# First layer's routing, row turning and scatter moved inside the recurrence, one block of 128 tokens per turn, with the turns of all engines written out

## Chip, core and metric

The kernel runs on one core of one Trainium2 chip. The metric is the device time of one execution in microseconds (us). TensorE is PE (its weight loads PEld), VectorE is DVE, ScalarE is ACT, GpSimd is POOL, SyncE is SP.

## What is computed

Four layers on x (8 batches, 512 tokens, 256 features). Only the first layer matters here: a recurrence (GRU) over 512 time steps, whose hidden states are the input of a mixture of 8 experts, two of which work on each token. The rest is cut.

```python
def step(h, inp):                       # _L0_cond_ref, scanned over t = 0..511, h is 8 x 256
    x_t, prop = inp
    comb = jnp.concatenate([x_t, h], axis=-1)
    z = jax.nn.sigmoid(comb @ Wz + bz)
    r = jax.nn.sigmoid(comb @ Wr + br)
    comb2 = jnp.concatenate([x_t, r * h], axis=-1)
    h_cand = jnp.tanh(comb2 @ Wh + bh)
    h_new = (1.0 - z) * h + z * h_cand
    h_next = jnp.where(prop, jnp.tanh(h_new @ Wp + bp), h_new)   # prop: every 4th step
    return (h_next, h_new)
# _L0_ffn_ref: logits = y @ gate_w + gate_b, the two largest of 8 per token, softmax of the two,
# out = sum of gate * (gelu(y @ w1[e] + b1[e]) @ w2[e] + b2[e]) over the token's two experts
x = x + _L0_ffn_ref(_L0_cond_ref(x, cond_1024, ...), ...)
x = x + _L1_ffn_ref(_L1_cond_ref(x, ...), ...)   # and two more layers
```

## The kernel before, in words

Everything lies in one program with a block per engine; the order on each engine is the order in the code, and semaphores join the engines.

**Recurrence.** 512 steps, in 32 turns (TURNS) of 16 (STEPS). Hidden states are kept with the features on the partitions, so a step's moving operand is 8 columns wide (the batches). Each value is held as two f16 parts. In one step PE multiplies h by the weights of gates r and z (`recur`, 24 matmuls, line 1546), ACT takes the tanh of r and of z (L669, L671), DVE makes r times h in parts (L996, L997, L999) and the mixing factors (L1002, L1003, L1005), PE does the candidate (12 matmuls), ACT its tanh (L673), and DVE's scan L1012 makes the new h, L1013 the same in f32 into `hist`, L1015 the low part. Each fourth step (CHUNK) adds a fourth product, an ACT tanh (L678) and `split_entry` (L983, L984, L986). While PE waits for c, it does one piece of the next turn's input projections (`projections`: a bias matmul, L1526 or L1534, or an f32 product with x, L1530). PE's turns are written out in the program; those of DVE, ACT (two at a time) and POOL are hardware loops (Fori). POOL copies `hist`, half a turn at a time, to HT, features by token (L588).

**After the recurrence.** PE makes the gate logits of all 4096 tokens from HT (`logits0`, L1590) and turns them (L1600). DVE picks the two experts for all 32 blocks of 128 tokens at once (`top2`, L1026 to L1032); two matmuls with a strict triangle and with ones count the ranks (`prefixes`); DVE makes `slots`, each token's two rows in the DRAM array tile_rows (L1070 to L1080), and `tile_table` makes `etab`, which tells SP what expert and rows each of the 39 tiles of 256 rows has (L1037 to L1051). Per block, PE turns 128 tokens of HT to rows (L1619), ACT copies them twice into `row_out0` (L719, L720, a ring of GRING = 4 blocks), and POOL scatters them by `slots` with two indirect DMAs (L611). SP waits for all 64 scatters and for `etab`, and loads the first tile's rows (L430) and weights (L389 to L392); then the expert tiles begin (L1654, L1666, with L731 on ACT). In the order of DVE, the router preparation for the second layer (L1084 to L1101) stands between `tile_table` and the expert tiles.

tile_rows is filled with zeros first, by 34 large DMAs of SP (L423, L424), 17 for each of two layers, which count to one semaphore, `xg_zeroed`.

## Time and profile before

| | us |
|---|---|
| median of 3 runs | 3123.79 (3120.74 to 3123.80) |
| profiled execution, its own time | 3125.09 |
| span of its trace | 3123.3 |
| recurrence, step 0 to the last | about 37 to 1293 |
| from there to the first expert matmul | 1293 to 1429 |
| PE busy / DVE busy / ACT busy / POOL busy | 2734.3 / 1386.6 / 863.7 / 406.7 |

The profiled execution is 1.3 us above the median. Its times are from the start of the span. A busy PE in the recurrence is a chain of dependent small matmuls, so the shares of busy time don't say what bounds; the waits do.

### The profile page before, as it was taken

The page shows a single profiled execution, that of the slowest core. Times are in us where ns is not written, and L with a number is a line of the kernel's source. Part 1 is how long each engine was busy: PE and PEld are TensorE (multiplying, and loading weights), DVE is VectorE, ACT ScalarE, POOL GpSimd, SP SyncE. Part 2 cuts the span into 40 slices and gives each one's busy share as a digit, 9 for nine tenths or more (in the row PEclk, how much of TensorE's full clock was granted, in tenths as well). Part 3 has the DMA queues.
Part 4 walks back from the last instruction along what each step waited for, and adds up shares of the span by engine and source line. Part 5 has one row for each costly group of instructions (what it writes and reads, how often), then busy time and mean ns, then how long its engine had stood idle before and what let it go on. Part 6 is the DMA issues. An engine that isn't in the chain of part 4 may idle for free.

```text
span 3123.3 us, 72740 instructions
## 1 busy us (share of the span) xinstructions
PE 2734.3 (88%) x27762; PEld 2069.9 (66%) x27762; DVE 1386.6 (44%) x6799; ACT 863.7 (28%) x2717; POOL 406.7 (13%) x478
## 2 busy tenths in 40 slices
PE   7888888888888888727999999899997999998788
PEld 5777777777777777516888888655784334386477
DVE  5555555555555555400111111366443556743532
ACT  1222222222222222222222222111353332433332
POOL 1000000000000000061111111122341000002233
PEclk6555555555555555658999999899998999999889
DMA  9990000000000000025666666521345321000123
GB/s 314 385 359 23 2 2 2 2 2 2 2 2 2 2 2 2 1 99 182 186 202 189 198 193 196 178 84 57 108 139 182 114 101 56 1 0 0 36 81 101
DMA packets 218189, 295.93 MB, mean 95 GB/s; under 512 B 57673, under 2 KB 160689, under 8 KB 216689
## 3 DMA queue, kind: packets, MB, share of 16 engines
q1 hardware_dynamic: 200624, 243.80, 23.9%
q0 software_dynamic: 17344, 48.78, 4.3%
q8 instruction: 188, 3.08, 0.4%
q14 instruction: 33, 0.26, 0.0%
HBM read 167.59 MB, written 124.94 MB: 94 GB/s over the span
## 4 chain that ended last, share of the span: by engine, by line
PE 76%; DVE 8%; ACT 6%; issue 5%; POOL 3%; DMA 2%; SPq 1%; DVEq 0%; POOLq 0%; ACTq 0%
PE bank L1546 20%; PE bank L1654 9%; PE bank L1666 9%; PE bank L1530 8%; PE bank L1738 4%; ACT gate_r L669 3%; DVE rhpart L996 3%; PE bank L1836 3%; PE bank L1880 3%; PE bank L1938 3%; PE bank L1789 2%; PE bank L1800 2%; POOL tile_rows L611 2%; PE bank L2036 2%; PE bank L2048 2%
## 5 line engine op out<-in xcount | busy, mean ns | idle before, releaser
L1546 PE MATMUL bank<-h_high,WB 128*128 128x8 f16 x9216 | 422.2, 169 | 87.2 <-DVE h_high L1012 67.4
L1546 PEld LDWEIGHTS bank<-h_high,WB 128*128 128x128 f16 x9216 | 335.5, 105 | 204.4 <-DVE h_high L1012 165.9
L1546 PE MATMUL bank<-rhpart,WB 128*128 128x8 f16 x6144 | 288.8, 171 | 84.8 <-DVE rhpart L996 84.8
L1546 PEld LDWEIGHTS bank<-rhpart,WB 128*128 128x128 f16 x6144 | 242.9, 106 | 130.7 <-DVE rhpart L996 128.1
L1654 PE MATMUL bank<-WA,WB 128*128 128x256 f32 x1248 | 310.1, 381 | 7.3 <-DMA WA<-in_L_ffn_b 7.3
L1666 PE MATMUL bank<-WB,hid 128*128 128x256 f32 x1248 | 313.8, 379 | 0.0
L1530 PE MATMUL bank<-XT,WB 128*128 128x128 f32 x792 | 304.6, 481 | 0.0
L1546 PE MATMUL bank<-h_low,WB 128*128 128x8 f16 x4608 | 299.7, 171 | 0.0
L1654 PEld LDWEIGHTS bank<-WA,WB 128*128 128x128 f32 x1248 | 238.7, 191 | 40.6 <-issue 7.7
L731 ACT ACTIVATE hid<-bank,b_up 128x256 f32<-128x256 f32 x312 | 148.0, 474 | 395.6 <-PE bank L1654 395.6
L1666 PEld LDWEIGHTS bank<-WB,hid 128*128 128x128 f32 x1248 | 234.3, 190 | 30.3
L1109 DVE TENSOR_TENSOR y_dest<-WA,pad_row 128x2 uint32<-128x2 f32 x78 | 12.5, 161 | 509.1 <-PE bank L1641 509.1
L669 ACT ACTIVATE gate_r<-bank 128x16 f32<-128x16 f32 x512 | 94.2, 184 | 495.8 <-PE bank L1546 495.8
L598 POOL DMA_INDIRECT expert_rows<-WA,y_dest x156 | 149.6, 959 | 592.1 <-DVE WA L1133 489.3
L1546 PEld LDWEIGHTS bank<-h_low,WB 128*128 128x128 f16 x4608 | 212.9, 106 | 17.3
L1530 PEld LDWEIGHTS bank<-XT,WB 128*128 128x128 f32 x792 | 198.7, 312 | 0.7
L588 POOL TENSOR_TENSOR HT<-GB,unscale 128x128 f32 x64 | 29.8, 466 | 1254.5 <-DVE GB L1013 1254.5
L1012 DVE TENSOR_TENSOR_SCAN h_high<-mix_times,mix_plus 128x32 f16<-128x32 f32 x512 | 115.2, 225 | 152.0 <-ACT mix_plus L673 152.0
L673 ACT ACTIVATE mix_plus<-bank 128x16 f32<-128x16 f32 x512 | 95.4, 186 | 279.4 <-PE bank L1546 279.4
L996 DVE SCALAR_TENSOR_TENSOR rhpart<-gate_r,GB 128x16 f16<-128x16 f32 x384 | 67.3, 175 | 223.0 <-ACT gate_r L669 223.0
L1880 PE MATMUL bank<-hid,WA 128*128 128x512 f32 x256 | 121.2, 607 | 0.0
L1836 PE MATMUL bank<-HT,WA 128*128 128x512 f32 x256 | 119.7, 593 | 0.0
(357 smaller groups left out, 3953.2 us busy)
## 6 DMA issues: line engine op xcount, KB each, us to landing
WB<-in_L_ffn_w SPq DMA_DIRECT2D x78, 1024.0 KB, 7.7
tile_rows<-WA SPq DMA_DIRECT2D x32, 2176.0 KB, 19.4
WA<-tile_rows SPq DMA_DIRECT2D x78, 272.0 KB
GB<-gates SPq DMA_DIRECT2D x8, 2048.0 KB
WA<-expert_rows SPq DMA_DIRECT2D x16, 512.0 KB, 5.4
WB<-expert_rows SPq DMA_DIRECT2D x16, 512.0 KB, 8.3
WA<-in_L_ffn_b SPq DMA_DIRECT2D x40, 128.0 KB, 8.2
GB<-in_x SPq DMA_DIRECT2D x8, 512.0 KB, 7.5
```

Of the source, the lines that this page charges most:

```text
L598: nc.gpsimd.indirect_dma_start(yg, bass.IndirectOffsetOnAxis(ap=y_dest[:, x, s:s + 1], axis=0), yrow[:, x % 2, s], None).then_inc(yrow_sto ...
L669: nc.scalar.activation(flat(gate_r), gate_in(r_bank, s), ACT.Tanh, scale=0.5 / GSCALE).then_inc(r_ready, 1)
L731: nc.scalar.activation(hid0[:, f], banks[f % RING][:, 0:ET], ACT.Gelu, bias=b0_up[:, i, f:f + 1]).then_inc(S["hid_ready"], 1)
L996: nc.vector.scalar_tensor_tensor(rhpart[:, 0], gate_r[:], 1.0, h, ALU.add, ALU.mult).then_inc(rh_part, 1)
L1012: nc.vector.tensor_tensor_scan(h_high[:], mix_times[:], mix_plus[:], 0.0, ALU.mult, ALU.add).then_inc(h_part, 1)
L1530: nc.tensor.matmul(o, wx[:, g, k, m * P:(m + 1) * P], xview[:, k, bass.ds(it * STEPS, STEPS)], start=False, stop=False, skip_group_check=True)
L1546: last = nc.tensor.matmul(bank[:, m * width + s * B:m * width + (s + 1) * B], wpart[:, g, w, k, m * P:(m + 1) * P], part[a][:, k * B:(k + ...
L1654: last = nc.tensor.matmul(banks[f % RING][:, 0:ET], w0_up[i][:, k, f * P:(f + 1) * P], xgT[:, i, k], start=k == 0, stop=k == KD - 1)
L1666: last = nc.tensor.matmul(banks[4 + m][:, 0:D], hid0[:, h, half_of(m)], w0_down[i][:, h], start=h == 0, stop=h == F0 - 1)
L1738: last = nc.tensor.matmul(banks[u % RING][:], (wsh1, wsh3)[u % 2][:, k, u // 2 * P:(u // 2 + 1) * P], XT[:, k, cols(j)], start=k == 0, sto ...
L1836: last = nc.tensor.matmul(banks[f % RING][:], v1[:, f, k], HT[:, k, cols(j)], start=k == 0, stop=k == KD - 1)
L1880: last = nc.tensor.matmul(banks[4 + m][:], v2[:, h, half_of(m)], hid[:, h % RING], start=False, stop=h == E - 1)
```

## The change

The work that followed the recurrence is done block by block inside it. A block is now one turn: 16 steps times 8 batches are 128 tokens, so their order in the blocks is another one (`dest_turn` holds the place of each in the result). In turn `it` the engines work on block `it - 1`:

- POOL makes two copies of each half turn, to HT as before and to `hturn` (in `hid`, a ring of two blocks), and scatters block `it - 2` at the turn's start. The first four scatters are held until turn 5.
- PE does the block's logits in steps 2 and 3 with `hturn` as weights, turns its rows in steps 6 and 7, and the two rank products in steps 12 and 13, all in spare columns of the bank that holds the fourth product. The projection pieces are dealt out anew, so that these steps have a bias piece and not an f32 one.
- DVE does the choice and the placing in pieces of one to three instructions behind steps 4 to 8, 12, 14, 15 and the next turn's step 0, on operands of 8 elements or fewer. `r_base` carries the counts from block to block.
- ACT copies the rows in step 8 and does one tanh in step 11 (the two gates are now a sigmoid of the difference of the two logits, where they were made with an exponential).
- The loops of DVE, ACT and POOL are written out, so their semaphore values are constants. DVE waits for the small loads (`rw_loaded`) and for POOL's constants ahead of the recurrence. POOL makes two more iotas at the start.
- Each layer's zero fill has a semaphore of its own. Behind the recurrence only block 31, the rest of block 30, `tile_table` and the second layer's preparation are left.

The diff, cut to its core (names of semaphores that only count on from another number are left out):

```diff
@@ POOL
-            with pool.Fori(0, TURNS) as it:
+            def scatter_block(b):
+                q = b % GRING
+                pool.wait_ge(slots_ready, b + 1)
+                pool.wait_ge(row_ready, b + 1)
+                for c in range(2):
+                    nc.gpsimd.indirect_dma_start(xg[0], bass.IndirectOffsetOnAxis(ap=slots[:, c, b:b + 1], axis=0),
+                                                 row_out0[:, q, c], None).then_inc(moved[q], 16)
+            def history(it, half):
...
+                if it >= 2:
+                    pool.wait_ge(row_psum, it - 1)
+                pool.wait_ge(h_full, it * STEPS + (half + 1) * n)
+                nc.gpsimd.tensor_tensor(hturn[:, it % 2].rearrange("p k (s b) -> p s k b", b=B)[:, half * n:(half + 1) * n], made, unscale[:],
+                                        ALU.mult).then_inc(hist_copied, 1)
+                nc.gpsimd.tensor_tensor(hview[:, it * STEPS + half * n:it * STEPS + (half + 1) * n], made, unscale[:],
+                                        ALU.mult).then_inc(hist_copied, 1)
+            for it in range(TURNS):
+                if it == GRING + 1:
+                    pool.wait_ge(xg_zeroed[0], ZEROED[0])
+                    for b in range(GRING - 1):
+                        scatter_block(b)
+                if it > GRING:
+                    scatter_block(it - 2)
                 for half in range(2):
+                    history(it, half)
+            for b in range(TURNS - 2, NBLK):
+                scatter_block(b)
@@ ACT, in gru_turn
+                    if it and s == 8:
+                        block_rows(it - 1, p_bank[:, 128:128 + D])
+                    if it and s == 11:
+                        block_gate(it - 1)
@@ DVE
+            def route_block(b, logit_bank, rank_bank, total_bank):
+                q = b % GRING
+                dve.wait_ge(logit_psum, b + 1)
+                V.tensor_tensor(r_log, logit_bank, rbias0[:], ALU.add).then_inc(logits_taken, 1)
+                yield
+                x = r_log
+                for m, mask in ((r_m1, r_mask1), (r_m2, r_mask2)):
...
+                    routed(V.tensor_reduce(m, x, AX_X, ALU.max))
+                    yield
+                    last_routed()
+                    routed(V.scalar_tensor_tensor(r_tmp, x, m, prefer[:], ALU.is_equal, ALU.mult))
+                    yield
+                    last_routed()
+                    routed(V.tensor_reduce(r_p, r_tmp, AX_X, ALU.max))
+                    yield
+                    last_routed()
+                    routed(V.tensor_scalar(mask, r_tmp, r_p, None, ALU.is_equal))
+                    yield
...
+                V.tensor_tensor(r_w, r_mask1, r_mask2, ALU.add).then_inc(masks_ready, 1)
...
+                dve.wait_ge(prefix_psum, b + 1)
+                routed(V.tensor_tensor(r_pos, rank_bank, r_base[:], ALU.add))
...
+            ROUTE_AT = {4: 3, 5: 3, 6: 3, 7: 3, 8: 1, 12: 1, 14: 3, 15: 3}
...
-            with dve.Fori(0, TURNS) as it:
+            dve.wait_ge(rw_loaded, 9 * 16)
+            dve.wait_ge(prefer_ready, 2 * E + 7)
+            dve.wait_ge(const_ready, 11)
...
+            for it in range(TURNS):
+                if it:
+                    routes.append(route_turn(it))
                 for s in range(STEPS):
...
+                    if s == 0 and len(routes) > 1:
+                        for _ in routes[-2]:
+                            pass
+                    if it:
+                        for _ in range(ROUTE_AT.get(s, 0)):
+                            next(routes[-1], None)
@@ PE
+            def beside_step(it, s, bias, inputs, p_bank):
+                if it + 1 < TURNS:
+                    for g, m in {0: ((0, 0), (0, 1)), 2: ((1, 0),), 3: ((1, 1),), 6: ((2, 0),), 7: ((2, 1),), 12: ((3, 0),), 13: ((3, 1),)}.get(s, ()):
+                        bias(g, m)
+                    for g, m, k in {1: ((0, 0, 0),), 4: ((0, 1, 0),), 5: ((0, 1, 1),), 8: ((1, 0, 1),), 9: ((1, 1, 0),), 10: ((1, 1, 1),),
+                                    11: ((2, 0, 0),), 14: ((2, 1, 0),)}.get(s, ()):
+                        inputs(g, m, k)
+                if it:
+                    b = it - 1
+                    if s in (2, 3):
+                        block_logits(b, p_bank[:, 64:64 + E], s - 2, False)
+                    if s in (6, 7):
+                        block_turn(b, p_bank[:, 128:128 + D], s - 6, False)
+                    if s == 12:
+                        block_ranks(b, p_bank[:, 72:72 + E], strict, False)
+                    if s == 13:
+                        block_ranks(b, p_bank[:, 80:80 + E], ones, False)
```

On PE, step 2 of a turn with a block, between the candidate's products and the next step's. Before, with one projection piece (L1530):

```order
L1546 MATMUL bank<-rhpart,WB 128x8 [waits rh_part]
L1546 MATMUL bank<-rhpart,WB 128x8 x3
L1530 MATMUL bank<-XT,WB 128x128
L1546 MATMUL bank<-h_high,WB 128x8 [waits h_part]
L1546 MATMUL bank<-h_high,WB 128x8 x7
```

and now (L1636 is `recur`, L1619 the bias piece, L1646 the logits with `hturn`, here under the name hid, as weights):

```order
L1636 MATMUL bank<-rhpart,WB 128x8 [waits rh_part]
L1636 MATMUL bank<-rhpart,WB 128x8 x3
L1619 MATMUL bank<-WA 128x128
L1646 MATMUL bank<-rw,hid 128x8 [waits rw_loaded,hist_copied]
L1636 MATMUL bank<-h_high,WB 128x8 [waits h_part]
L1636 MATMUL bank<-h_high,WB 128x8 x7
```

The f32 projection has gone to another step, and a bias piece and an f32 product with 8 columns stand there, the latter behind POOL's copies.

On DVE, the end of step 4 and the start of step 5. Before:

```order
L1012 SCALAR_TENSOR_TENSOR h_high<-mix_times,mix_plus 128x32 [waits mix_ready,c_ready]
L1013 SCALAR_TENSOR_TENSOR GB<-mix_times,mix_plus 128x32
L1015 TENSOR_TENSOR h_low<-GB,h_high 128x16 [waits h_full]
L995 REGISTER_ALU
L996 SCALAR_TENSOR_TENSOR rhpart<-gate_r,GB 128x16 [waits r_ready]
```

and now (L1123, L1124, L1126 and L1107 are the same four instructions; r_all holds the routing's small operands):

```order
L1123 SCALAR_TENSOR_TENSOR h_high<-mix_times,mix_plus 128x32 [waits mix_ready,c_ready]
L1124 SCALAR_TENSOR_TENSOR GB<-mix_times,mix_plus 128x32
L1126 TENSOR_TENSOR h_low<-GB,h_high 128x16 [waits h_full]
L1019 TENSOR_TENSOR r_all<-bank,rbias 128x8 [waits logit_psum]
L1027 TENSOR_REDUCE r_all<-r_all 128x1 [waits logits_taken]
L1030 SCALAR_TENSOR_TENSOR r_all<-r_all,prefer 128x8 [waits place_step]
L1107 SCALAR_TENSOR_TENSOR rhpart<-gate_r,GB 128x16 [waits r_ready]
```

Three instructions, of which each waits for the one before, have come between the low part and the next step's first instruction; the register instruction is gone.

On POOL, the two halves of a turn. Before, in the loop:

```order
L588 ISA [waits h_full]
L588 TENSOR_TENSOR HT<-GB,unscale 128x8x16
L587 REGISTER_ALU
L588 ISA [waits h_full]
L588 TENSOR_TENSOR HT<-GB,unscale 128x8x16
```

and now (hid is `hturn`):

```order
L603 TENSOR_TENSOR hid<-GB,unscale 128x8x2x8 [waits h_full,row_psum]
L605 TENSOR_TENSOR HT<-GB,unscale 128x8x16
L603 TENSOR_TENSOR hid<-GB,unscale 128x8x2x8 [waits h_full,row_psum]
L605 TENSOR_TENSOR HT<-GB,unscale 128x8x16
L593 DMA tile_rows<-GB,slots 33024x272 [waits row_ready,slots_ready,xg_zeroed0]
L593 DMA tile_rows<-GB,slots 33024x272
```

Each half turn has two copies, one straight behind the other, and from turn 5 on scatters stand between the turns.

## Rows read from the trace of the kernel before

**Rows 1.** The page: granted clock in 40 slices; instruction queue: packets, MB, share.

```profile
PEclk6555555555555555658999999899998999999889
q8 instruction: 188, 3.08, 0.4%
```

**Rows 2.** Windows: start:end, length, busy us and count of each engine, clock, DMA share, GB/s.

```profile
37.00:1293.00 1256.00, 1084.03 (x20994) 899.35 (x20993) 693.33 (x4989) 307.15 (x1663) 29.63 (x64) 0.50 0.17 62
1334.00:1416.00 82.00, 19.75 (x62) 9.03 (x61) 0.38 (x3) 19.92 (x59) 61.61 (x64) 0.50 0.29 109
```

**Rows 3.** Timeline of plain steps in turn 1: start, us, what, idle before.

```profile
78.26 0.23 DVE L1012 TENSOR_TENSOR_SCAN h_high<-mix_times,mix_plus 128x32 f16<-128x32 f32 x1 [0.38 <-ACT mix_plus L673]
...
79.18 0.18 ACT L669 ACTIVATE gate_r<-bank 128x16 f32<-128x16 f32 x1 [1.04 <-PE bank L1546]
...
80.02 0.50 PEld L1530 LDWEIGHTS bank<-XT,WB 128*128 128x128 f32 x2
...
80.44 0.23 DVE L1012 TENSOR_TENSOR_SCAN h_high<-mix_times,mix_plus 128x32 f16<-128x32 f32 x1 [0.28 <-ACT mix_plus L673]
...
80.72 0.29 PEld L1546 LDWEIGHTS bank<-h_high,WB 128*128 128x128 f16 x8 [0.20 <-DVE h_high L1012]
...
80.82 0.18 DVE L1015 TENSOR_TENSOR h_low<-GB,h_high 128x16 f16<-128x16 f32 x1
...
81.36 0.18 ACT L669 ACTIVATE gate_r<-bank 128x16 f32<-128x16 f32 x1 [0.95 <-PE bank L1546]
...
81.57 0.17 DVE L996 SCALAR_TENSOR_TENSOR rhpart<-gate_r,GB 128x16 f16<-128x16 f32 x1 [0.58 <-ACT gate_r L669]
```

**Rows 4.** Timeline at the eighth step of a turn: POOL's copy and split_entry.

```profile
291.44 0.47 POOL L588 TENSOR_TENSOR HT<-GB,unscale 128x128 f32 x1 [19.18 <-DVE GB L1013]
292.05 0.18 DVE L983 TENSOR_SCALAR h_high<-entry 128x16 f16<-128x16 f32 x1 [0.58 <-ACT entry L678]
292.14 0.17 DVE L984 TENSOR_SCALAR entry_s<-entry 128x16 f32<-128x16 f32 x1
```

**Rows 5.** Timeline near 2870 to 2890: DVE beside POOL's back-to-back adds.

```profile
2870.04 19.65 POOL L631 TENSOR_TENSOR XT<-XT,GB 128x512 f32 x16 [174.07 <-ACT GB L906]
...
2885.52 4.20 DVE L1409 TENSOR_SCALAR ys<-condT 128x16 f32<-128x16 f32 x1
```

**Rows 6.** Timeline: DVE L1459 during POOL's issue of a DMA, then without.

```profile
2943.69 0.29 DVE L1459 TENSOR_SCALAR sgate<-sgate 128x4 f32<-128x4 f32 x1
...
2966.36 0.17 DVE L1459 TENSOR_SCALAR sgate<-sgate 128x4 f32<-128x4 f32 x1
```

**Rows 7.** Timeline of PE's first projections: a bias piece, then f32 pieces.

```profile
30.10 0.10 PEld L1526 LDWEIGHTS bank<-WA 2*128 2x128 f16 x1 [0.23 <-issue]
...
30.31 0.93 PEld L1530 LDWEIGHTS bank<-XT,WB 128*128 128x128 f32 x4
```

**Rows 8.** Timeline of DVE: small instructions, each waiting for the one before.

```profile
2011.27 0.17 DVE L1209 TENSOR_SCALAR q_all<-q_all 128x4 f32<-128x4 f32 x1
2011.47 0.18 DVE L1210 RECIPROCAL q_all<-q_all 128x4 f32<-128x4 f32 x1
```

**Rows 9.** Timeline from the last step to the first row copy.

```profile
1292.72 0.47 POOL L588 TENSOR_TENSOR HT<-GB,unscale 128x128 f32 x1 [19.17 <-DVE GB L1013]
...
1327.95 0.28 DVE L1037 TENSOR_TENSOR GB<-GB,tile_first 1x128 f32<-1x128 f32 x1
...
1331.24 0.19 DVE L1051 CAST etab<-etab_f 1x78 uint32<-1x78 f32 x1
...
1332.61 0.57 ACT L720 COPY GB<-bank 128x512 f32<-128x512 f32 x1
```

**Rows 10.** The chain of waits around the last scatter: start, us, what.

```profile
1413.99 2.43 DMA tile_rows<-GB,slots
...
1417.49 0.41 SPq L430
...
1420.49 8.14 DMA WA<-in_L_ffn_b
```

More of the change, by code:

```diff
@@ L663, in flat, with both, block_rows, block_gate @@
                 return x[:].rearrange("p (k b) -> p k b", k=KD)
+            def both(x):
+                return x.rearrange("p (a d) -> p a d", a=1).to_broadcast([P, 2, D])
+            def block_rows(b, bank):
+                q = b % GRING
+                act.wait_ge(row_psum, b + 1)
+                if b >= GRING:
+                    act.wait_ge(moved[q], 32 * (b // GRING))
+                nc.scalar.copy(row_out0[:, q, :, MW:], both(bank)).then_inc(row_ready, 1)
+            def block_gate(b):
+                act.wait_ge(score_in, b + 1)
+                nc.scalar.activation(r_t, r_d, ACT.Tanh, scale=0.5).then_inc(score_th, 1)
             def gru_turn(it, r_bank, z_bank, c_bank, p_bank):
@@ L991, in _ @@
+            routes = []
+            for it in range(TURNS):
+                if it:
+                    routes.append(route_turn(it))
                 for s in range(STEPS):
@@ L1077, in _ @@
[L1077 to L1082 removed]
+            dve.wait_ge(ranks_taken, NBLK)
+            link(V.tensor_tensor(t_all, r_base[0:1], region[0:1], ALU.subtract))
@@ L1550, in recur, with block_logits, block_turn @@
                 return last
+            def block_logits(b, o, k, first):
+                if k == 0:
+                    pe.wait_ge(hist_copied, 4 * b + 8)
+                    pe.wait_ge(rw_loaded, 9 * 16)
+                i = nc.tensor.matmul(o, hturn[:, b % 2, k], rw[:, 0, k, 0:E],
+                                     start=first and k == 0, stop=k == KD - 1, skip_group_check=True)
+                if k == KD - 1:
+                    i.then_inc(logit_psum, 1)
+            def block_turn(b, o, k, first):
+                if k == 0 and not first:
+                    pe.wait_ge(logits_taken, b + 1)
+                i = nc.tensor.matmul(o[:, k * P:(k + 1) * P], hturn[:, b % 2, k], ident[:],
+                                     start=first and k == 0, stop=k == KD - 1, is_transpose=True, skip_group_check=True)
+                if k == KD - 1:
+                    i.then_inc(row_psum, 1)
@@ new lines, in block_ranks @@
+            def block_ranks(b, o, w, first):
+                if w is strict:
+                    pe.wait_ge(masks_ready, b + 1)
+                    if not first:
+                        pe.wait_ge(row_ready, b + 1)
+                i = nc.tensor.matmul(o, w[:], r_w, start=first, stop=True, skip_group_check=True)
+                if w is ones:
+                    i.then_inc(prefix_psum, 1)
+            def beside_step(it, s, bias, inputs, p_bank):
[15 more added lines that the diff above has]
+                        block_ranks(b, p_bank[:, 80:80 + E], ones, False)
@@ L1564, in gru_turn @@
                     recur(gates[2], 2, W, s, rh_parts, lambda a: pe.wait_ge(rh_part, n * 2 + a + 1)).then_inc(c_psum, 1)
-                    next(following, None)
+                    beside_step(it, s, bias, inputs, gates[3])
                     if (s + 1) % CHUNK == 0:
+                        if it and s == STEPS - 1:
+                            pe.wait_ge(ranks_taken, it)
+                        if it and s == 11:
+                            pe.wait_ge(row_ready, it)
                         recur(gates[3], 3, NP * B, s // CHUNK, h_parts,
                               lambda a: pe.wait_ge(h_part, n * 2 + a + 1)).then_inc(p_psum, 1)
-                        next(following, None)
-                for _ in following:
-                    pass
-            for _ in projections(0, *banks[0:4]):
-                pass
+                        beside_chunk(it, s, inputs)
+            bias, inputs = projections(0, *banks[0:4])
+            for g in range(4):
+                for m in range(KD):
+                    bias(g, m)
+                    if g < 3:
+                        for k in range(KD):
+                            inputs(g, m, k)
             for it in range(TURNS):
@@ L1613, in _ @@
[L1613 to L1623 removed]
+            pe.wait_ge(cent_ready, 2)
             for k in range(KD):
```

305 lines of the change are left out of this document (142 added, 163 removed).

## The prediction

> **What bounds the kernel now.** I read the page's slices first, then a table of windows, then the timeline of single steps, then the chain of waits behind the recurrence. The slices show TensorE's clock at its lower level, 1.2 GHz (half), for the whole recurrence [rows 1]. The windows give it 1256 us for 32 turns, 39.25 us a turn, 0.50 granted clock, and behind it a stretch of 82 us in which POOL is busy 61.6 us and PE 19.8 [rows 2].
>
> Inside a step the reader should look at the gaps. A plain step is 81.36 - 79.18 = 2.18 us from gate_r to gate_r. DVE's low part L1015 starts at 80.82, the next DVE instruction L996 at 81.57, held by gate_r; the gap is 0.58 us. ACT is idle 0.95 us ahead of gate_r. PE's projection piece starts its weights at 80.02, and the next step's first weights come at 80.72, held by the scan; 0.20 us of that are idle [rows 3]. So a step is one dependent chain, and each engine has a hole. What goes into a hole costs nothing as long as it ends in time.
>
> Behind the recurrence the chain is serial: POOL's last copy at 1292.72, logits, choice, ranks, slots, table, then 64 scatters. The last scatter, issued at 1413.99, lands 2.43 us later, and SP issues the first tile's rows at 1417.49 [rows 9, 10]. The experts then start behind an 8.14 us load [rows 10]. That part stays as it is.
>
> **Term 1, the tail.** Before, it runs from 1292.72 to SP's load at 1417.49, 124.8 us. After, with the same zero:
> - POOL makes two copies where it made one: 0.47 each, so 1293.63.
> - Two f32 logit products, weights of 128x128 in two passes, 0.50 each as in the projection piece [rows 3]: 1294.7.
> - DVE's choice, 11 instructions that wait for each other. The pitch of such small ones is 2011.47 - 2011.27 = 0.20 us [rows 8]; I take 0.21 for operands of 8: 2.3 us, 1297.0.
> - Two rank products, again 0.50 each: 1298.1.
> - Placing, 8 instructions, 1.7 us: 1299.8.
> - Now two paths. POOL issues two scatters 1.3 us apart (64 in 82 us, [rows 2]), and the last lands 2.43 us after its issue [rows 10]: 1299.9 + 1.3 + 2.4 = 1303.6. DVE makes the tile table, 1331.43 - 1327.95 = 3.5 us [rows 9], plus a subtraction: 1303.5.
> - SP's first load comes 1417.49 - 1416.42 = 1.07 us behind the landing [rows 10]: 1304.7.
>
> The gain is 1417.49 - 1304.7 = 112.8 us. Block 30's scatters need 2.6 us and are issued from about 1295, ahead of block 31's slots. The second layer's preparation, which lay under the scatters, now lies under the 8.14 us weight load. It is some twelve small instructions of DVE, ACT and PE in a row, by the pitch of 0.2 us and PE's 0.5 us pieces an estimated 5 us from 1303.5; with no cover it would cost those 5. Bounds: 100 if each link takes double, 115 if POOL's second copy doesn't count.
>
> **Term 2, DVE's pieces.** Six steps of a turn (4, 5, 6, 7, 14, 15) have up to three linked instructions. Starting 0.09 behind L1015, they begin at 80.91, 81.11, 81.32 and end at 81.49; L996 is due at 81.57 [rows 3, 8]. I take 0, but the margin is only 0.08. Lower bound 0, upper bound a pitch of 0.23 and a late start, 0.1 us a step: 6 x 31 x 0.1 = 19 us. Behind a late L996 stand PE's candidate products, so all of it would count.
>
> **Term 3, PE's pieces.** Steps 2, 3, 12 and 13 have a bias piece and an f32 product. From a bias piece's weights to the next weights is 0.21 us [rows 7], the f32 weights take 0.50: 0.71 us from 80.02, where the hole is 0.70 [rows 3]. I take 0.02 us late: 4 x 31 x 0.02 = 2.5 us. Upper bound 0.15 each, 19 us, lower bound 0. The other pieces are single and as before, or a bias piece with a turn of one pass, which is shorter. The rank products wait for ACT's copy of step 8 and DVE's masks of step 7, both steps old.
>
> **Term 4, ACT.** The row copy takes 0.57 us [rows 9] in a hole of 0.95 [rows 3], the one-column tanh less. Zero; without the hole it would be 31 x 0.57 = 18 us.
>
> **Term 5, POOL beside DVE.** This speaks against the change. A DVE tensor_scalar of 128x16 f32 (L1409), which elsewhere takes 0.17, took 4.20 us while POOL worked through its back-to-back adds, from 2885.52 to 2889.72; POOL's row ends at 2889.69 [rows 5]. L983 and L984 of split_entry are of that kind, and stand on the path. Today POOL's copy ends at 291.44 + 0.47 = 291.91, and L983 starts at 292.05: clear. The second copy will run until 292.34, so L983 would end at 292.37 where it ends at 292.23 now: 0.14 us [rows 4]. Twice a turn, 64 x 0.14 = 9.0 us. Lower bound 0 (L983 writes f16, and is not exactly L1409's form), upper bound 0.3 each, if it only begins at the release: 19 us. I take 9.0. SBUF — State Buffer in the Trainium skill, section Who interferes with whom, says that such an instruction and a GpSimd one exclude each other for the whole instruction, and counts a tensor_tensor with two SBUF inputs beside a GpSimd read too. By that rule L986 is hit as well, but it comes after the release, so the sum would be the same 9 us; the trace agrees with the lock by its 4.20 us.
>
> POOL's scatters fall in steps 1 and 2 of a turn. A small DVE instruction during the issue of a DMA took 0.29 us for 0.17 [rows 6]. L1002 and L1003 can be hit so, but the scan behind them waits for ACT with 0.28 us idle [rows 3]. Zero.
>
> **Term 6, loops written out.** In steps 0 and 8 the scan, which there also waits for POOL with a computed value, has 0.38 us idle ahead of it where others have 0.28 [rows 3]. At most 64 x 0.10 = 6.4 us come back, at least 0, since the third wait stays; I take 3.
>
> **Term 7, the start.** Two more iotas delay POOL, and DVE waits for small loads ahead of step 0. DVE is idle before the recurrence while PE does its first projections. Zero.
>
> **Sum.** The recurrence gets 2.5 + 9.0 - 3 = 8.5 us longer, the tail 112.8 shorter: 3125.1 - 104.3 = 3020.8 for an execution like the profiled one. The median stands 1.3 us below that one: **3019.5 us**. The experts and later layers do the same work on the same numbers of tiles.
>
> **Rivals.**
> - *The steps stretch.* DVE's linked pieces don't fit, PE's pieces run over, and the lock costs its upper bound: 19 + 19 + 19 = 57 us at worst. With about half of that beyond my sum, 30 us, the time is 3050. For it: margins of 0.08 and -0.01 us. Against it: DVE's and PE's pieces are priced from rows of their own kind. 0.18.
> - *No lock, all waits gone.* Terms 3 and 5 are zero and term 6 is 6: 3123.8 - 112.8 - 6 = 3005. 0.10.
> - *Slower than before.* The written-out streams of DVE and ACT don't reach their engines in time. The steps would have to lose the whole gain: from 112.8 / 512 = 0.22 us a step on, a tenth of a step, the kernel is slower, and at 0.3 us a step it would be 3123.8 - 112.8 + 154 = 3165. Against it: PE's turns are written out already, 36 small products a step, and the steps still take 2.18 us; the instruction queue moved 3.08 MB in 188 packets in all [rows 1]. Runtime: NRT & Kernel Launch in the Trainium skill, section Instruction fetch mechanics, says that sequential fetching is mostly hidden and branches are what breaks it; no row here prices a fetch. 0.04.
> - *The change doesn't do what it says*: the scatters stay serial behind the recurrence, because a block's slots or rows are late by a ring. 64 x 1.3 = 83 us of the gain stay away: 3019.5 + 83 = 3103. The waits look one or more turns back, so 0.02.
> - *TensorE's clock.* The recurrence gets denser by the block's products. If the clock rose to 2.4 GHz in it, hundreds of us would go. Nothing in the rows shows it: PE was busy 1084 of 1256 us at half clock [rows 2]. 0.02.
>
> My forecast, 3010 to 3033, has 0.64.
>
> **Numbers.** Forecast, no-lock case and most of the stretching case lie in 3002 to 3056; I leave out the rest, about 0.15. A difference of 0.2%, 6 us, is about what a measurement of this kernel can tell from none. Faster 0.95, the same 0.01, slower 0.04.
>
> **What would show it.** Right: SP's first row load about 12 us behind the last step; L1000 (the former L983) long, about 0.3 us, in steps 7 and 15; turns of 39.5 us. Term 2 is wrong if L1107 starts late in steps 4 to 7, 14 and 15, term 3 if the first h_high weights come more than 0.28 us behind the scan in steps 2, 3, 12 and 13. The prediction as a whole falls if a turn is over 41 us, or if POOL still issues scatters long after the last step.

## The result, and the profile after

| | before | after |
|---|---|---|
| median, us | 3123.80 (3120.74 to 3124.76, 4 runs) | 3011.39 (3009.92 to 3013.29, 4 runs) |
| profiled execution / its span | 3125.09 / 3123.3 | 3010.22 / 3008.4 |
| first to last gate_r of the recurrence | 1253.31 | 1252.02 |
| POOL's first copy after the last step to SP's first row load | 124.77 | 12.31 |
| SP's first row load to the first expert matmul | 11.36 | 11.39 |
| first expert matmul to the end | 1694.45 | 1693.29 |

The ratio is 0.964, with a 95% interval of 0.9628 to 0.9651. The predicted time was 8.1 us too high, all of it outside the tail. Three executions below took 6506, 3997 and 7495 us, where the others of their kernels agree within 0.3%, and are left out of every median here.

The page of the changed kernel: the clock in 40 slices, then the second of the two instruction queues. The first row stands against [rows 1]: the clock is at its lower level for as long as the recurrence lasts, as before, and rises one slice earlier in the span, since the tail is gone. The 6 of the 17th slice before was 17 us at the full level in the old tail (1297.4 to 1314.5, PE busy 15.2 of them); the new tail has none. In the page of the kernel before, q14 had 33 packets and 0.26 MB.

```profile
PEclk6555555555555555579999999999998999999999
...
q14 instruction: 91, 0.75, 0.1%
```

Windows of the changed kernel (length, busy us and count of PE, PEld, DVE, ACT, POOL, then clock, DMA share, GB/s): the recurrence, the tail, and the first six us of the experts.

```profile
37.00:1292.00 1255.00, 1133.69 (x21273) 954.01 (x21272) 787.95 (x5697) 323.57 (x1726) 115.39 (x188) 0.50 0.19 69
1292.00:1303.00 11.00, 2.54 (x10) 2.07 (x10) 9.05 (x45) 0.81 (x3) 4.18 (x5) 0.50 0.14 51
1315.00:1318.00 3.00, 2.89 (x7) 2.36 (x8) 0.00 (x0) 1.76 (x2) 0.00 (x0) 0.50 0.87 298
1318.00:1321.00 3.00, 3.00 (x16) 2.64 (x15) 0.00 (x0) 0.95 (x2) 0.00 (x0) 0.99 1.06 358
```

Against [rows 2], the recurrence took in 50 us more of PE, 95 of DVE and 86 of POOL without becoming longer, and the 82 us stretch with 61.6 of POOL is gone. In the tail it is now DVE that is busy, 9.05 of 11 us.

The tail in the timeline of the changed kernel. The reader should follow who releases whom: logits (L1646), choice (L1019 to L1044), ranks (L1666), slots (L1072), scatters (L593), table (L1170), load (L428).

```profile
1291.41 0.46 POOL L603 TENSOR_TENSOR hid<-GB,unscale 128x128 f32<-128x128 f32 x1 [18.77 <-DVE GB L1124]
1291.83 0.47 POOL L605 TENSOR_TENSOR HT<-GB,unscale 128x128 f32<-128x128 f32 x1
...
1292.37 0.93 PEld L1646 LDWEIGHTS bank<-rw,hid 128*128 128x128 f32 x4 [0.65 <-ACT entry L719]
...
1293.43 0.17 DVE L1019 TENSOR_TENSOR r_all<-bank,rbias 128x8 f32<-128x8 f32 x1
...
1293.73 1.01 POOL L593 DMA_INDIRECT tile_rows<-GB,slots  x1 [1.43 <-DVE slots L1072]
...
1294.09 0.16 DVE L1033 TENSOR_REDUCE r_all<-r_all 128x1 f32<-128x8 f32 x1
1294.28 0.43 DVE L1036 TENSOR_SCALAR r_all<-r_all 128x8 f32<-128x8 f32 x1
...
1295.04 0.96 POOL L593 DMA_INDIRECT tile_rows<-GB,slots  x1 [0.30 <-issue]
...
1295.60 0.38 DVE L1036 TENSOR_SCALAR r_all<-r_all 128x8 f32<-128x8 f32 x1
1296.01 0.17 DVE L1044 TENSOR_TENSOR r_all<-r_all 128x8 f32<-128x8 f32 x1
...
1296.61 0.55 PEld L1666 LDWEIGHTS bank<-r_all,ones 128*128 128x128 f32 x2
...
1298.54 0.15 DVE L1072 CAST slots<-r_all 128x1 uint32<-128x1 f32 x1
...
1300.23 0.96 POOL L593 DMA_INDIRECT tile_rows<-GB,slots  x1 [0.30 <-issue]
...
1302.21 0.19 DVE L1170 CAST etab<-etab_f 1x78 uint32<-1x78 f32 x1
...
1303.72 0.42 SPq L428 DMA_DIRECT2D WA<-tile_rows  x1
```

Two of the choice's instructions (L1036) are long, 0.43 and 0.38 for 0.22: both end with POOL's issue of a DMA (1294.74 and 1296.00), while the reduction L1033 just ahead of each, also beside an issue, keeps its 0.16.

For the recurrence I took the starts of gate_r in the trace and the distance from each to the next. This is the median of each step's distance (step s to s + 1) over the turns, and the number of steps more than 0.04 us above their median.

| us | steps 0, 8 | plain | 3, 11 | 7, 15 | long ones, their excess | 512 steps |
|---|---|---|---|---|---|---|
| before | 2.28, 2.27 | 2.18 | 3.22 | 3.22 | 0 | 1253.31 |
| after | 2.17, 2.18 | 2.18 | 3.22 | 3.31 | 17, 2.11 | 1252.02 |

So two things moved: steps 0 and 8 lost 0.10 us, and 7 and 15 gained 0.09. The long steps are of two kinds. In 13 of the 17 one of DVE's two scans starts late (experiment 2). In the other four, 55, 81, 82 and 83, with 0.45 us in all, DVE instructions take longer beside POOL. Step 55 has a low part of `split_entry` (L1003) held by a copy. The other three lie in turn 5, where POOL issues the eight scatters of blocks 0 to 3 in a row, from 233.2 to 243.3. This is step 83:

```profile
242.29 0.96 POOL L593 DMA_INDIRECT tile_rows<-GB,slots  x1 [0.30 <-issue]
...
242.80 0.43 DVE L1000 TENSOR_SCALAR h_high<-entry 128x16 f16<-128x16 f32 x1 [0.58 <-ACT entry L719]
```

L1000 ends at 243.23, with the issue.

Here is a chunk's end, step 7 of a turn of the changed kernel, against [rows 4]:

```profile
291.27 0.46 POOL L603 TENSOR_TENSOR hid<-GB,unscale 128x128 f32<-128x128 f32 x1 [13.42 <-PE bank L1655]
291.68 0.47 POOL L605 TENSOR_TENSOR HT<-GB,unscale 128x128 f32<-128x128 f32 x1
291.90 0.28 DVE L1000 TENSOR_SCALAR h_high<-entry 128x16 f16<-128x16 f32 x1 [0.58 <-ACT entry L719]
292.09 0.16 DVE L1001 TENSOR_SCALAR entry_s<-entry 128x16 f32<-128x16 f32 x1
...
292.29 0.17 DVE L1003 TENSOR_TENSOR h_low<-entry_s,h_high 128x16 f16<-128x16 f32 x1
```

POOL's second copy ends at 292.15; L1000, due to end at 292.08, ends at 292.18. Turns 0 and 1 show the same thing with another dose: there POOL has no wait for `row_psum`, its first copy starts 0.28 behind the scan L1124 and not 0.34 to 0.35, L1000 takes 0.22, and the steps take 3.24 to 3.25.

### The profile page after: what moved, and what is told of

Its sections match the earlier page's. It is cut to its first block, busy times and chain, and to the rows that moved or that the text cites. A ratio compares the mean times of both kernels' runs of the same rounds, so it can differ in the third digit from the quotient of the medians.

```text
span 3008.4 us, 72385 instructions
## 1 busy us (share of the span) xinstructions
PE 2742.4 (91%) x27918; PEld 2107.5 (70%) x27918; DVE 1475.0 (49%) x7505; ACT 853.5 (28%) x2708; POOL 435.3 (14%) x544
## 4 chain that ended last, share of the span: by engine, by line
PE 81%; DVE 7%; ACT 5%; issue 4%; DMA 1%; POOL 1%; SPq 1%; POOLq 0%; DVEq 0%; ACTq 0%
PE bank L1636 20%; PE bank L1772 9%; PE bank L1784 9%; PE bank L1623 8%; PE bank L1856 3%; ACT gate_r L706 3%; DVE rhpart L1107 3%; PE bank L1954 3%; PE bank L1998 3%; PE bank L2056 3%; PE bank L1907 2%; PE bank L1918 2%; PE bank L2154 2%; PE bank L2166 2%; PE bank L1865 2%
## 5 line engine op out<-in xcount | busy, mean ns | idle before, releaser
L1636 PE MATMUL bank<-h_high,WB 128*128 128x8 f16 x9216 | 419.7, 169 | 36.4 <-DVE h_high L1123 33.9
L1636 PEld LDWEIGHTS bank<-h_high,WB 128*128 128x128 f16 x9216 | 337.9, 105 | 137.1 <-DVE h_high L1123 80.9
L1636 PE MATMUL bank<-rhpart,WB 128*128 128x8 f16 x6144 | 287.8, 171 | 84.5 <-DVE rhpart L1107 84.5
L1636 PEld LDWEIGHTS bank<-rhpart,WB 128*128 128x128 f16 x6144 | 242.2, 106 | 130.1 <-DVE rhpart L1107 127.8
L1636 PE MATMUL bank<-h_low,WB 128*128 128x8 f16 x4608 | 298.9, 171 | 0.3
L1623 PE MATMUL bank<-XT,WB 128*128 128x128 f32 x768 | 295.3, 481 | 0.0
L1636 PEld LDWEIGHTS bank<-h_low,WB 128*128 128x128 f16 x4608 | 212.1, 106 | 13.6 <-DVE h_low L1126 0.2
L1123 DVE TENSOR_TENSOR_SCAN h_high<-mix_times,mix_plus 128x32 f16<-128x32 f32 x512 | 114.9, 224 | 146.3 <-ACT mix_plus L710 146.2
L603 POOL TENSOR_TENSOR hid<-GB,unscale 128x128 f32<-128x128 f32 x64 | 29.3, 458 | 1078.3 <-DVE GB L1124 690.5
L1107 DVE SCALAR_TENSOR_TENSOR rhpart<-gate_r,GB 128x16 f16<-128x16 f32 x384 | 67.1, 175 | 147.6 <-ACT gate_r L706 143.4
```

Source lines behind the costliest of these rows:

```text
L1107: nc.vector.scalar_tensor_tensor(rhpart[:, 0], gate_r[:], 1.0, h, ALU.add, ALU.mult).then_inc(rh_part, 1)
L1123: nc.vector.tensor_tensor_scan(h_high[:], mix_times[:], mix_plus[:], 0.0, ALU.mult, ALU.add).then_inc(h_part, 1)
L1623: nc.tensor.matmul(gate_banks[g][:, m * W:(m + 1) * W], wx[:, g, k, m * P:(m + 1) * P], xview[:, k, bass.ds(it * STEPS, STEPS)], start=Fal ...
L1636: last = nc.tensor.matmul(bank[:, m * width + s * B:m * width + (s + 1) * B], wpart[:, g, w, k, m * P:(m + 1) * P], part[a][:, k * B:(k + ...
```

## Theories and experiments

My theory after the result: (a) the tail's gain is the scatters and the choice that left it; (b) the steps hide all new pieces but the second copy, which holds `split_entry`; (c) the written-out streams give back what steps 0 and 8 lost, and pay with some long steps. Rivals: to (b), that the recurrence is longer because of the new pieces themselves, or that the 0.09 has to do with the step and not with the copy; to (c), that the change of the pieces made steps 0 and 8 shorter. The runs shared the chip with runs of the kernel before, whose median is given. Where one execution stands alone, traces of the same recurrence differ by 0.3% (1253.31, 1249.78 and 1249.04 us in the kernel before and in two versions whose DVE loop is the same), and the first gate_r comes anywhere from 37.5 to 40.8 us, so distances inside one trace weigh more than spans.

**1. The loops alone.** The kernel before, with

```diff
-            with pool.Fori(0, TURNS) as it:
+            for it in range(TURNS):
-            with act.Fori(0, TURNS // 2) as it2:
+            for it2 in range(TURNS // 2):
-            with dve.Fori(0, TURNS) as it:
+            for it in range(TURNS):
```

> The kernel before, with only its recurrence loops on DVE, ACT and POOL written out; nothing else of the change. In the trace of the changed kernel the steps 0 and 8 of a turn take 2.18 us, where they took 2.28 and 2.27 before, and steps 7 and 15 take 3.31 where they took 3.22. Theory 1 (what steps 0 and 8 lost was the wait with a computed value): here too steps 0 and 8 take 2.18 us, 7 and 15 stay at 3.22, and the span falls by 64 x 0.095 = 6.1 us, to 3117.2. Rival (the written-out streams cost something in return, by late instructions): steps outside this pattern grow, and the span falls by less than 3 us. The scattered long steps of the changed kernel (17 of 512, 2.1 us in all) also come here if the written-out streams make them, and don't if the routing work does.

Measured: 3116.68 median (10 runs) against 3122.78, ratio 0.998 (0.9971 to 0.9989). Steps 0 and 8 take 2.18 us. So about 6 us (3.4 to 9.1 by the interval) can be had from the loops alone, and have nothing to do with routing. But eight steps of the 512 are now 0.1 to 0.2 us long, 1.05 us in all, of which the kernel before has none. q14 moved 0.69 MB.

**2. Which engine's loop.** Two more versions, each with one of the three lines: DVE's alone, and ACT's alone.

> The kernel before with only DVE's recurrence loop written out (ACT and POOL keep their loops). Question 1, the 0.10 us that steps 0 and 8 lose: the scan there waits for POOL with a value computed in a register by DVE, so they should be 2.18 here as with all loops written out (64 x 0.10 = 6.2 us less, median 3117.5). Question 2, the eight long steps of 512 (0.1 to 0.2 us each, 1.05 us in all) that appeared with all loops written out, in which DVE's scan starts 0.46 instead of 0.28 us behind ACT's last end: if DVE's own stream makes them, they are here, at the same steps; rival: they come from ACT's stream, whose signal is late, and are absent here.

> The kernel before with only ACT's recurrence loop written out. Steps 0 and 8 should stay at 2.28 us and the time at 3123.8. If DVE's stream makes the long steps, none is here; rival: they come from ACT's stream and are here, at the same steps as with all loops written out (98, 217 and 336, 119 steps apart, among them).

Measured: DVE's alone 3115.90 against 3121.93, ratio 0.998 (0.997 to 0.9989), steps 0 and 8 at 2.18, and the same eight long steps: 86, 98, 205, 217, 324, 336, 479 and 491 in both traces. ACT's alone 3122.96, ratio 1.0004 (0.9994 to 1.0014), steps 0 and 8 at 2.27 and 2.26, no long step. Both the gain and the long steps are DVE's. The timeline of step 98 of the version with DVE's loop written out:

```profile
277.28 0.19 ACT L673 ACTIVATE mix_plus<-bank 128x16 f32<-128x16 f32 x1 [0.55 <-PE bank L1546]
277.67 0.23 DVE L1012 TENSOR_TENSOR_SCAN h_high<-mix_times,mix_plus 128x32 f16<-128x32 f32 x1 [0.46 <-ACT mix_plus L673]
```

The scan starts 0.20 us behind the end of what it waits for, where others start some 0.03 behind it. What makes it late can be read from its place. I count DVE's records in the trace from 0, those of its sequencer (waits and register instructions) included. In both versions the late scans (the first, L1012, or the second, L1013) are records 1008, 1136, 2288, 2416, 3568, 3696, 5232 and 5360. In the changed kernel the 13 late scans are in steps 2, 14, 56, 109, 130, 172, 214, 235, 277, 445, 466, 487 and 508, records 112 to 6256; the trace in 6 has the same 13. Every one of these numbers is 112 plus a multiple of 128. The converse holds too: wherever such a number falls on one of the two scans, that scan is late, 8 of 8 and 13 of 13, and where it falls on another instruction no step is long.

Queue q14 moves packets of 8192 bytes, 40 more of them with DVE's loop written out (33 with loops, 73 with DVE's written out, 43 with ACT's), and there are 43 such numbers in DVE's recurrence; with DVE's alone written out one packet starts 0.66 to 0.94 us behind each of the eight late scans. So the late scans stand where DVE's stream goes over to its next 128 instructions, and the queue's packets come in step with that. How the loading of one block holds a scan, nobody varied: that link is argued.

Why steps 0 and 8 gain is in the same records. In the loop, L1011, the third wait's value, is a register instruction of 0.04 to 0.05 us that stands behind the wait for c: in step 32 of the kernel before it starts at 117.44, 0.03 behind ACT's end, and the scan 0.09 behind it. Written out, L1011 is a plain wait that stands ahead of the wait for c (116.68 in step 32 of experiment 1's version, where the scan starts at 117.13), in time in which DVE waits anyway.

**3. The second copy away.** Nothing reads what the changed kernel copies to HT in the recurrence. This version leaves that copy out:

```diff
-            pool.sem_inc(hist_copied, 2)
...
-                nc.gpsimd.tensor_tensor(hview[:, it * STEPS + half * n:it * STEPS + (half + 1) * n], made, unscale[:],
-                                        ALU.mult).then_inc(hist_copied, 1)
...
-                        dve.wait_ge(hist_copied, (it * 2 + 1 + s // (STEPS // 2)) * 2)
+                        dve.wait_ge(hist_copied, it * 2 + 1 + s // (STEPS // 2))
...
-                    pe.wait_ge(hist_copied, 4 * b + 8)
+                    pe.wait_ge(hist_copied, 2 * b + 4)
```

> The changed kernel without POOL's second copy of each half turn, the one to HT, which nothing reads before it is overwritten. Theory 1 (that copy holds DVE's L1000, the first of split_entry, in steps 7 and 15, which take 0.09 us longer than steps 3 and 11): they fall to 3.22 us, L1000 to 0.18 us everywhere, the span falls by 64 x 0.09 = 5.8 us, to 3002.6, and the time to about 3005.6. Rival (the 0.09 us is DVE's own linked pieces or PE's pieces in these steps): they stay at 3.31 us and the span at 3008.4.

Measured: 3005.26 (5 runs) against 3122.78, ratio 0.962 (0.9608 to 0.9633). Steps 7 and 15 take 3.23, as 3 and 11 do. That is (b), and not a property of those steps.

**4. A third copy.** The same value once more, to spare columns of `hid`:

```diff
+                nc.gpsimd.tensor_tensor(hidf[:, 512 + it % 2 * 256 + half * 128:512 + it % 2 * 256 + half * 128 + 128].rearrange("p (s k b) -> p s k b", k=KD, b=B), made, unscale[:],
+                                        ALU.mult).then_inc(hist_copied, 1)
```

> The changed kernel with a third copy of each half turn on POOL, to a spare place. The third ends 0.42 us behind the second. Theory 1 (a lock held for each POOL instruction, and POOL's next one follows before DVE gets in): L1000 in steps 7 and 15 ends 0.42 us later still, and steps 7 and 15 take 3.73 us; span +27 us, 3035. Theory 1b (DVE gets in between the second and the third copy): steps 7 and 15 as in the changed kernel, span about 3008 to 3012. Rival (POOL has nothing to do with it): 3008.4.

Measured, in one execution: span 3023.6; steps 7 and 15 at 3.46, which is 0.15 over the changed kernel and 0.24 over a step without a hold. These are 9.3 of the 15.2 us; 2.2 are a later start. Neither of my theories gave that. The timeline at such a step (lines are three further down):

```profile
295.78 0.47 POOL L606 TENSOR_TENSOR HT<-GB,unscale 128x128 f32<-128x128 f32 x1
...
296.00 0.28 DVE L1003 TENSOR_SCALAR h_high<-entry 128x16 f16<-128x16 f32 x1 [0.58 <-ACT entry L722]
296.19 0.16 DVE L1004 TENSOR_SCALAR entry_s<-entry 128x16 f32<-128x16 f32 x1
296.21 0.46 POOL L608 TENSOR_TENSOR hid<-GB,unscale 128x128 f32<-128x128 f32 x1
...
296.38 0.32 DVE L1006 TENSOR_TENSOR h_low<-entry_s,h_high 128x16 f16<-128x16 f32 x1
```

The high part is held by the second copy, as in the changed kernel (0.28). Then DVE gets in at the change from the second copy to the third: L1004 is not held. The low part is held in its turn, 0.32 instead of 0.17, until the third copy ends (296.67). So here each hold ends with one POOL instruction, and a row of them holds one DVE instruction after another, when these come one by one. That is no rule: L1409 in [rows 5] was held over several adds, and step 87 of the trace in 5 has another case, below. What decides whether DVE gets in at a change stays open. L1006 is a tensor_tensor with two inputs in SBUF, L1033 of the tail a reduction. SBUF — State Buffer in the Trainium skill, section Who interferes with whom, says that the first kind is held by a GpSimd instruction that reads SBUF and that a tensor_reduce never is; the traces agree, with 0.32 for 0.17 and 0.16 for 0.16.

**5. Scatters twice, in both kernels.** Each block is scattered a second time, to a spare array:

```diff
-                for c in range(2):
-                    nc.gpsimd.indirect_dma_start(xg[0], bass.IndirectOffsetOnAxis(ap=slots[:, c, b:b + 1], axis=0),
+                for d, c in ((xg[0], 0), (xg[0], 1), (spare, 0), (spare, 1)):
+                    nc.gpsimd.indirect_dma_start(d, bass.IndirectOffsetOnAxis(ap=slots[:, c, b:b + 1], axis=0),
```

> The kernel before with each scatter of the first layer issued a second time, to a spare array of the same size. Theory (behind the recurrence each of POOL's 64 scatters costs its issue, 1.26 us, in the open): span +64 x 1.26 = 81 us, 3204. Rival (the stretch is paced by the landing and by the ring of row_out0, not by the issue): much less than 81 us, or more if landings queue.

> The changed kernel with each scatter of the first layer issued a second time, to a spare array. Theory (in the recurrence POOL's issue is hidden): only the tail grows, by two issues of 1.26 us, and by DVE instructions that POOL's DMA issue holds, 0.1 to 0.3 us each, where they now fall on the path; span +2.5 to +10 us, 3011 to 3018. Rival (DVE pays for POOL's DMA issues in the recurrence): one issue more in each of steps 2 and 3 of 27 turns costs 0.1 to 0.3 us each: up to +16 us.

Measured in the kernel before: span 3201.1, and from POOL's last copy to SP's load 1494.23 - 1288.35 = 205.9 us where it was 124.8. These are 81.1 us for 64 scatters, 1.27 each. In the changed kernel: span 3017.2, 8.7 us more; 3.1 of them lie ahead of the recurrence, 1.5 in it, 2.6 in the tail and 1.5 behind it. Of the 1.5 in the recurrence 1.0 are one step, 87. POOL's row of issues in turn 5, now sixteen, reaches its `split_entry`, and the copies follow at once:

```profile
255.61 0.96 POOL L594 DMA_INDIRECT spare_rows<-GB,slots  x1 [0.30 <-issue]
...
255.95 1.15 DVE L1001 TENSOR_SCALAR h_high<-entry 128x16 f16<-128x16 f32 x1 [0.58 <-ACT entry L720]
...
256.60 0.47 POOL L604 TENSOR_TENSOR hid<-GB,unscale 128x128 f32<-128x128 f32 x1
```

L1001 begins during the issue, isn't let in at its end (256.57), and ends at 257.10 with the first copy (257.06): one hold over two POOL instructions. The timeline of the tail:

```profile
1296.06 0.46 POOL L604 TENSOR_TENSOR hid<-GB,unscale 128x128 f32<-128x128 f32 x1 [18.77 <-DVE GB L1125]
...
1302.21 0.96 POOL L594 DMA_INDIRECT spare_rows<-GB,slots  x1 [0.30 <-issue]
1303.65 0.95 POOL L594 DMA_INDIRECT tile_rows<-GB,slots  x1 [0.48 <-DVE slots L1073]
...
1307.45 0.96 POOL L594 DMA_INDIRECT spare_rows<-GB,slots  x1 [0.30 <-issue]
1310.95 0.42 SPq L429 DMA_DIRECT2D WA<-tile_rows  x1
```

Of 64 scatters more, 60 are hidden in the recurrence; the two more of block 31 lengthen the tail by 2.6, which is 2 x 1.3. With 81 us in the one kernel and 2.6 in the other's tail, the scatters are shown to be off the path, all but block 31's two, which still end it: the last one lands and SP's load follows.

**6. The changed kernel and the one without the second copy on one chip.**

> The changed kernel itself, for a comparison on one chip with the version without the second copy. The copy's cost read inside one trace is (3.31 - 3.22) us in steps 7 and 15 of 31 turns, 62 x 0.09 = 5.6 us. So this one should stand 5.6 us above the version without the copy; rival: the 5.3 us between the two medians of different chips was chance, and the two are within 2 us of each other. Absolute: 3011.

> The changed kernel without POOL's copy of the history to HT, which no instruction reads, on the same chip as the changed kernel. Expected 3005.5, 5.6 us below it (steps 7 and 15 at 3.22 to 3.23 as 3 and 11); rival: within 2 us of it.

Measured: 3010.40 (5 runs, 3009.34 to 3013.28) and 3005.58 (5 runs, 3004.04 to 3006.20), with before at 3124.3; ratios 0.9641 (0.9628 to 0.9653) and 0.9621 (0.9608 to 0.9634). The runs don't overlap. The second copy costs 4.8 us, and 1252.20 - 1247.52 = 4.7 us lie in the recurrence. The same place in the trace of the version without it, three lines further up:

```profile
290.34 0.46 POOL L602 TENSOR_TENSOR hid<-GB,unscale 128x128 f32<-128x128 f32 x1 [13.43 <-PE bank L1652]
...
290.98 0.18 DVE L997 TENSOR_SCALAR h_high<-entry 128x16 f16<-128x16 f32 x1 [0.58 <-ACT entry L716]
```

This is the fastest version of the study.

**7. Is there room left in DVE's hole?** The routing's instructions in larger pieces, five to a step in three steps:

```diff
-            ROUTE_AT = {4: 3, 5: 3, 6: 3, 7: 3, 8: 1, 12: 1, 14: 3, 15: 3}
+            ROUTE_AT = {4: 5, 5: 5, 6: 2, 8: 1, 12: 1, 14: 5, 15: 3}
```

> The changed kernel with DVE's routing pieces dealt out in fives: five linked instructions behind steps 4, 5 and 14 where there were three, and none or fewer behind 6, 7 and 15. In the changed kernel DVE is idle 0.17 to 0.22 us ahead of the next step's first instruction in the steps with three. Two more are 0.40 us, so that one comes 0.2 to 0.25 us late: if the margin is a hard edge, steps 4, 5 and 14 take 2.40 us for 2.18, 3 x 31 x 0.22 = +20 us, span 3029. Rival (DVE is not what ends last there): 3008 still.

Measured, in one execution: span 3032.8, and 1274.31 - 1252.02 = 22.3 us more in the recurrence. Two steps of a turn take 2.50, 0.32 more, and step 15 0.07 more: 62 x 0.32 + 31 x 0.07 = 22.0. The 0.32 is more than I expected because I had the idle time wrong: ahead of L1107 it is 0.04 to 0.05 us in steps 5, 6 and 7 of the changed kernel, and 0.12 to 0.23 only in steps 0, 8 and 15. The timeline at the fifth step:

```profile
288.60 0.16 DVE L1019 TENSOR_TENSOR r_all<-bank,rbias 128x8 f32<-128x8 f32 x1
...
289.04 0.18 ACT L706 ACTIVATE gate_r<-bank 128x16 f32<-128x16 f32 x1 [0.94 <-PE bank L1636]
...
289.44 0.23 DVE L1036 TENSOR_SCALAR r_all<-r_all 128x8 f32<-128x8 f32 x1
289.58 0.17 DVE L1107 SCALAR_TENSOR_TENSOR rhpart<-gate_r,GB 128x16 f16<-128x16 f32 x1
289.80 0.48 PEld L1636 LDWEIGHTS bank<-rhpart,WB 128*128 128x128 f16 x12 [0.57 <-DVE rhpart L1107]
```

L1107 is due at 289.26, 0.04 behind gate_r's end, and starts at 289.58, 0.32 late, and PE's candidate products with it (0.57 idle for 0.25). All of a late L1107 counts, as term 2 had it. The five start 0.10 behind the low part's start and have a pitch of 0.19 to 0.26.

**8. Is there room left in PE's hole?** Both logit products in step 2:

```diff
-                    if s in (2, 3):
-                        block_logits(b, p_bank[:, 64:64 + E], s - 2, False)
+                    if s == 2:
+                        for k in range(KD):
+                            block_logits(b, p_bank[:, 64:64 + E], k, False)
```

> The changed kernel with both f32 logit products of a block in step 2, behind the bias piece, none in step 3. Steps 2, 3, 12 and 13 have shown no loss with 0.10 + 0.50 us of weights each. Theory (the hole is 0.70 us of weight loads and what is over it is late one for one): step 2 gets 0.21 + 0.50 + 0.50 = 1.21 us, 0.5 us over: 31 x 0.5 = +15.5 us, span 3024. Rival (some of it is absorbed, since the products themselves are short): less than +8 us.

Measured, in one execution: span 3025.2. That it is so near the expected 3024 is luck. Step 2 takes 2.53, 0.35 more and not 0.5, 31 x 0.35 = 10.9 us, between my theory and its rival; the other 6 us are a later start (0.7), steps that were a little longer all through this run (2.8) and 2.4 behind the recurrence. The timeline:

```profile
281.50 0.10 PEld L1619 LDWEIGHTS bank<-WA 2*128 2x128 f16 x1
...
281.72 0.93 PEld L1646 LDWEIGHTS bank<-rw,hid 128*128 128x128 f32 x4
...
281.83 0.22 DVE L1123 TENSOR_TENSOR_SCAN h_high<-mix_times,mix_plus 128x32 f16<-128x32 f32 x1 [0.28 <-ACT mix_plus L710]
...
282.38 0.32 PEld L1636 LDWEIGHTS bank<-h_high,WB 128*128 128x128 f16 x2
```

The next weights come 0.55 behind the scan's start, where they are due 0.28 behind it: a second f32 product of 0.46 to 0.50 doesn't fit behind the bias piece. That is 0.27 of the 0.35; the rest lies between these weights and their first product, which starts 0.22 behind them. One product alone fits, as the changed kernel shows at step 13:

```profile
1286.16 0.50 PEld L1666 LDWEIGHTS bank<-r_all,ones 128*128 128x128 f32 x2
...
1286.58 0.23 DVE L1123 TENSOR_TENSOR_SCAN h_high<-mix_times,mix_plus 128x32 f16<-128x32 f32 x1 [0.28 <-ACT mix_plus L710]
...
1286.86 0.29 PEld L1636 LDWEIGHTS bank<-h_high,WB 128*128 128x128 f16 x8 [0.20 <-DVE h_high L1123]
```

## Why the prediction was right, and where it missed

**Term 1, the tail: right.** Predicted 112.8, measured 124.77 - 12.31 = 112.46. With the same zero (+1.31 on the after trace): copies done 1293.61 for 1293.63, logits 1294.74 for 1294.7, choice 1297.5 for 1297.0, ranks 1298.6 for 1298.1, placing 1300.0 for 1299.8, table 1303.7 for 1303.5, load 1305.0 for 1304.7. Of the 0.5 that the choice is late, 0.37 are the two L1036 that block 30's scatters hold; I had priced that only for the steps. Experiment 5 shows the mechanism. That the second layer's preparation hides under the load is right: 11.39 for 11.36.

**Term 2, DVE's pieces: right, zero, with a margin even thinner than said.** L1107 still comes 0.03 behind gate_r's end in every step, but where three pieces stand ahead of it DVE is idle only 0.04 to 0.05 (steps 5, 6, 7), where I had 0.08; experiment 7 shows what the hole costs when it is overrun.

**Term 3, PE's pieces: 2.5 predicted, none measured.** The mis-sized part is the 0.02 a step: after a single f32 product the next weights are 0.28 behind the scan, as ever. Experiment 8 gives the price beyond it.

**Term 4 and term 7: right.** The copy of the rows leaves step 8 at 2.18, and the first gate_r comes at 37.65 for 37.64.

**Term 5, the lock: right in mechanism and place, 9.0 predicted, 5.4 measured by the steps (59 x 0.09 and 4 x 0.02), 4.8 by leaving the copy out on one chip.** The mis-sized part is the hold, 0.14 predicted and 0.09 to 0.10 measured, in two halves. I put the second copy's end 0.90 us behind the first's start (292.34 - 291.44; the "0.47 each" of term 1 would even be 0.94), and it is 0.88. And `split_entry` comes 0.63 to 0.65 behind the first copy where it came 0.61. What this term also put at nothing are the DMA issues: right for the scatters of steps 1 and 2, but the eight of turn 5 fall on `split_entry` and others, 0.35 us in steps 81 to 83.

**Term 6, written-out loops: 3 predicted, 6.2 measured.** I chose the middle of 0 and 6.4, on the thought that the third wait stays; the upper end was right. It stays, but ahead of the wait for c, where it costs nothing, and the register instruction behind that wait, which cost the 0.10, is gone (experiment 2). What the term lacked are the late scans, 13 steps with 1.7 of the 2.1 us. They are a small case of the rival with the late instructions: the direction was right, the size is 2 us, not 112. Runtime: NRT & Kernel Launch in the Trainium skill, section Instruction fetch mechanics, has sequential fetching as mostly hidden; if these are fetches, the traces agree, with 1 to 2 us in 1250.

**What no term had.** The experts are 1.2 us shorter: the clock reaches its full level 2.9 us behind their first matmul (at 1318.0) and not 5.1 us (at 1434.0). Before, in the columns of the windows above:

```profile
1432.00:1435.00 3.00, 3.00 (x11) 2.51 (x10) 0.00 (x0) 0.95 (x2) 0.00 (x0) 0.67 0.87 234
```

By an estimate from these, 2.2 us at twice the clock are worth 1.1. What brings it up earlier wasn't tried. And 2.5 us of the recurrence are left over, 0.005 us a step, which is no more than the 3.5 to 4.3 us by which traces of one recurrence differ; that it is this and nothing else isn't shown.

In sum, against the profiled execution: -3.2 (term 6), -3.6 (5), -2.5 (3), +2.1 (long steps), -2.5 (left over), +0.3 (1), -1.2 (experts) make -10.6, and 3020.8 - 10.6 = 3010.2. The left-over part is what the sum needs to close. That is the lower end of the case I forecast. Most of the misses point one way, so the range held because each of them is small, not because they cancel. The rival "no lock, all waits gone", 3005, is what the version without the second copy does, 3005.58, though that one too has the late scans.

## What to carry to other kernels

Work that stands serial behind a chain of dependent steps can go into the holes of the steps for nothing, as long as each piece ends before the engine's next instruction on the chain is due: measure the hole once, keep to it (three linked small DVE instructions, or one bias piece and one f32 product, here), since beyond it every tenth of a microsecond counts in each of the steps. Look for what the new work does to engines beside it: a POOL copy that nobody reads cost 4.8 us through DVE, which one trace shows, in the steps that have it against those that don't. When a few steps of many are long, count their instructions: a fixed distance in the stream told the late scans from the held ones here. And split the gain by cause: some 6 of 112 us can be had from loops written out alone, with DVE's loop alone.

## What the runs showed of the hardware

- A POOL tensor_tensor on SBUF holds a DVE tensor_scalar of 128x16 (0.28 for 0.18 us) and a tensor_tensor with two SBUF inputs (0.32 for 0.17) until a POOL instruction ends. In experiment 4 DVE got in at the change to the next one; in experiment 5 (1.15 us, step 87) and in [rows 5] (4.20 us) it didn't.
- POOL's issue of an indirect DMA held a tensor_scalar of 128x8 (0.43 and 0.38 for 0.22) and of 128x16 (0.43 for 0.18), and no reduction (0.16).
- In DVE's loop, a register instruction between its wait for c and the scan let the scan of steps 0 and 8 start 0.10 us later than with constants.
- In a written-out DVE stream a scan was 0.05 to 0.19 us late wherever it was the first of a new 128 instructions, 8 of 512 steps in one kernel and 13 in another, the same ones in each trace; q14's packets have 8192 bytes and keep step with these.
- Indirect DMAs of 128 rows have a pitch of 1.27 us on POOL whether to one array or to two.
